# One batch of roots in place of two in the second layer normalisation of a two-block metaformer kernel

## The reference

```python
x = x + _L0_conv_ref(_ln_c(x), ...)                 # block 1, with normalisation 0 over channels
t = _to_tokens(x)
t = t + _L0_ffn_ref(_ln_t(t), ...)                  # block 2, with normalisation 1 over channels
...
def _ln_t(v, eps=1e-05):
    m = jnp.mean(v, axis=-1, keepdims=True)
    s = jnp.var(v, axis=-1, keepdims=True)
    return (v - m) / jnp.sqrt(s + eps)
# in _L0_ffn_ref: one choice of two experts per image, from the mean over the image's tokens
logits = jnp.mean(x, axis=1) @ Wr + br
routing_weights = jax.nn.softmax(logits, axis=-1)
```

## Time and profile before

| | us |
|---|---|
| median of 3 timed runs | 288.39 |
| lowest and highest | 288.17, 289.09 |
| the profiled execution, its own time | 287.14 |
| its span, first to last instruction | 285.3 |
| PE, DVE, ACT busy in the span | 269.7, 156.7, 142.0 |

### The profile page before, as it was taken

One profiled execution on the slowest core, in us unless ns is written; L12 is line 12 of the kernel. 1 busy time (PEld: TensorE's weight loads), 2 busy tenths in 40 slices (PEclk: granted clock), 3 DMA queues, 4 the chain that ended last, 5 costly groups with the idle time before them and its releaser, 6 DMA issues.

```text
span 285.3 us, 6450 instructions
## 1 busy us (share of the span) xinstructions
PE 269.7 (95%) x2474; PEld 139.5 (49%) x2474; DVE 156.7 (55%) x357; ACT 142.0 (50%) x225; POOL 33.3 (12%) x74
## 2 busy tenths in 40 slices
PE   5899999999889898999899999999999999999993
PEld 4464444346665446757355434533344444444672
DVE  3676887787753385556635148473344444444444
ACT  3642242524358665046612355265555566666672
POOL 6224546400025200000000000000000000000000
PEclk9999999999999999999999999999999999999999
DMA  7716768770000000000008980000966900800010
GB/s 189 287 48 180 217 201 227 205 267 0 0 2 1 2 1 2 2 0 2 0 20 203 209 173 1 2 0 14 191 142 142 192 0 2 177 10 2 0 39 22
DMA packets 11566, 24.09 MB, mean 84 GB/s; under 512 B 2192, under 2 KB 4400, under 8 KB 11408
## 3 DMA queue, kind: packets, MB, share of 16 engines
q1 hardware_dynamic: 9808, 19.19, 27.2%
q0 software_dynamic: 1328, 3.84, 5.4%
q10 hardware_dynamic: 400, 0.66, 0.8%
HBM read 14.73 MB, written 1.33 MB: 56 GB/s over the span
## 4 chain that ended last, share of the span: by engine, by line
PE 82%; DVE 9%; ACT 3%; issue 3%; DMA 2%; DVEq 1%; ACTq 0%; POOLq 0%
PE PS L803 21%; PE PS L780 21%; PE PS L735 6%; PE PS L610 6%; PE PS L506 4%; PE PS L562 3%; PE PS L540 3%; PE PS L708 2%; PE PS L690 2%; PE PS L627 2%; PE PS L599 2%; PE PS L575 2%; DMA X<-x_in 2%; PE PS L634 2%; PE PS L749 2%
## 5 line engine op out<-in xcount | busy, mean ns | idle before, releaser
L780 PE MATMUL PS<-N,late 64*64 64x512 f32 (+1 forms) x640 | 70.8, 550 | 0.0
L942 ACT ACTIVATE amp<-PS,late 128x1024 f32<-128x1024 f32 (+1 forms) x40 | 39.0, 1025 | 32.2 <-PE PS L780 32.2
L942 ACT ACTIVATE h<-PS,late 128x1024 f32<-128x1024 f32 (+1 forms) x40 | 39.2, 1025 | 31.8 <-PE PS L780 31.8
L780 PEld LDWEIGHTS PS<-N,late 64*64 64x64 f32 x640 | 26.1, 133 | 32.5 <-issue 31.5
L803 PE MATMUL PS<-amp,late 64*64 64x512 f32 (+1 forms) x320 | 35.3, 549 | 0.0
L803 PE MATMUL PS<-h,late 64*64 64x512 f32 (+1 forms) x320 | 35.0, 548 | 0.0
L1297 DVE SCALAR_TENSOR_TENSOR D<-PS,late,moved 128x512 f32<-128x512 f32 (+1 forms) x24 | 14.8, 657 | 28.5 <-PE PS L803 23.0
L1297 DVE SCALAR_TENSOR_TENSOR D<-PS,late,gB_odd 128x512 f32<-128x512 f32 x16 | 11.3, 747 | 28.9 <-PE PS L803 28.9
L1303 DVE TENSOR_TENSOR X<-D,X 128x512 f32<-128x512 f32 (+1 forms) x40 | 25.3, 633 | 2.1
L407 POOL DMA_DIRECT2D moved<-amp x40 | 19.7, 497 | 26.7 <-DMA moved<-amp 13.3
L844 ACT ACTIVATE Q<-PS 128x384 f32<-128x384 f32 x24 | 11.6, 488 | 21.4 <-PE PS L506 21.3
(11 more groups left out here) (151 smaller groups left out, 290.2 us busy)
## 6 DMA issues: line engine op xcount, KB each, us to landing
gB_odd<-gates_hbm SPq DMA_DIRECT2D x4, 1024.0 KB, 13.6
moved<-amp SPq DMA_DIRECT2D x40, 96.0 KB, 3.2
moved<-amp POOLq DMA_DIRECT2D x35, 96.0 KB, 2.9
moved<-gates_hbm SPq DMA_DIRECT2D x4, 512.0 KB, 7.3
moved<-gates_hbm SPq DMA_DIRECT2D x2, 1024.0 KB, 9.7
late<-late_in SPq DMA_DIRECT2D x1, 1852.0 KB, 7.5
moved<-gates_hbm SPq DMA_DIRECT2D x4, 256.0 KB, 5.4
mix<-mix_in SPq DMA_DIRECT2D x1, 897.0 KB, 9.3
```

Source lines behind the costliest of these rows:

```text
L780: mm = pe.matmul(PS[64 * r:64 * r + 64, 2 * ring(n) + half, 0:w], L("w1")[rows, u:u + 64], N[rows, a:a + w], start=True, stop=True, skip_g ...
L942: act.activation(h2[n // 2 % 2][:, 2 * (n % 2):2 * (n % 2) + 2, 0:w], pair(ring(n), w), ACT.Gelu, bias=L("b1")[:, BLOCKS * g + b:BLOCKS * ...
```

## The change

The last two batches of normalisation 1 become one, of chunks 3, 4 and 5. Its sums stand in bank 6, where those of chunks 3 and 4 stood; bank 5 no longer holds any. ACT's list takes the squares of chunks 4 and 5 ahead of their copies, and the load of the Exp table stands behind the root of the new last batch. PE's list has six unread products of 256 columns behind the sums of that batch, where there were two, three of 128 columns between the spreads of chunks 4 and 5 no longer, and three of 256 columns in place of two behind the last spread.

```diff
-BATCHES = [[[0], [1, 2], [3, 4, 5]], [[0, 1, 2], [3, 4], [5]]] + [[[0, 1, 2], [3, 4, 5]]] * 3
+BATCHES = [[[0], [1, 2], [3, 4, 5]], [[0, 1, 2], [3, 4, 5]]] + [[[0, 1, 2], [3, 4, 5]]] * 3
-SUMS_BANK = [[6, 7, 0], [7, 6, 5]]
+SUMS_BANK = [[6, 7, 0], [7, 6]]
-ROOTED = [(0, 0), (0, 1), (0, 2), (1, 0), (1, 1), (1, 2), (2, 1), (3, 0), (3, 1), (4, 0)]
+ROOTED = [(0, 0), (0, 1), (0, 2), (1, 0), (1, 1), (2, 1), (3, 0), (3, 1), (4, 0)]
...
-        root 1 1, root 1 2, warm 2, spread 1 3, spread 1 4, unread 3, spread 1 5, warm 2, route_logits, warm 2, route_loads, warm 2, route_picks, warm 4,
+        root 1 1, warm 6, spread 1 3, spread 1 4, spread 1 5, warm 3, route_logits, warm 2, route_loads, warm 2, route_picks, warm 4,
...
-                if (i, b) == (1, 2):
+                if (i, b) == (1, 1):
                     load_table(ACT.Exp)
```

More of the change, by code:

```diff
@@ L201 @@
         l1 0, l1 1, products 0 3, amplify 3, products 1 3, fc 0, fc 1, amplify 4, l1 2, l1 3, products 2 3, amplify 5, products 3 3, fc 2, fc 3, moments 1 0,
-        moments 1 1, moments 1 2, l1 4, l1 5, root 1 0, products 4 3, products 5 3, fc 4, fc 5, moments 1 3, moments 1 4, moments 1 5, root 1 1, root 1 2,
+        moments 1 1, moments 1 2, l1 4, l1 5, root 1 0, products 4 3, products 5 3, fc 4, fc 5, moments 1 3, square 1 4, square 1 5, copy 1 4, copy 1 5, root 1 1,
         router, select 0, hidden0 0, select_scaled 0, hidden0 1, hidden0 2, hidden0 3, select 1, hidden0 4, hidden0 5, select_scaled 1, hidden0 6, hidden0 7,
@@ L214 @@
         shifted 34, shifted 35, shifted 36, shifted 37, fc 2, shifted 38, shifted 39, shifted 40, l1 5, shifted 41, shifted 42, shifted 43, shifted 44,
-        shifted 45, shifted 46, shifted 47, root 1 0, fc 3, spread_l1 4, spread 1 0, spread_l1 5, spread 1 1, spread 1 2, fc 4, fc 5, center_w2, root 1 1, root 1 2,
+        shifted 45, shifted 46, shifted 47, root 1 0, fc 3, spread_l1 4, spread 1 0, spread_l1 5, spread 1 1, spread 1 2, fc 4, fc 5, center_w2, root 1 1,
         spread 1 3, spread 1 4, spread 1 5, router, down0 0 1, down0 1 1, root 2 0, spread 2 0, spread 2 1, spread 2 2, down0 2 1, down0 3 1, root 3 0, spread 3 0, spread 3 1, spread 3 2, root 2 1, conv 0, spread 2 3,
```

## The result

The changed kernel is slower. Its median is 289.59 us over twelve runs (289.01 to 290.04), against 288.42 us over twelve of the kernel before; the ratio is 1.0034, with a 95% interval of 1.0022 to 1.0046, about 0.98 us. (The two medians themselves lie 1.17 us apart; the ratio carries the interval, so I go by it.) Forecast were 288.54 us and "the same", with a range up to 289.2: the time lies outside it.

A forecast was written before the change was run, and what follows sets the result against it. PE was taken to bound most of the kernel, but DVE's chain the changed place. Spreads waiting behind unread products add 0.15 us to the 288.39 us median, giving 288.54 us; range 287.7 to 289.2, "the same" at 0.85.

The forecast's parts named there:

- the start of the sums: Sums of the one batch of chunks 3, 4 and 5 start at 71.03 us; the last sums before started at 71.75.
- the roots: In the new batch: reciprocal at 72.34 us, `rows` at 73.64; spreads could start at 73.99, 0.26 us gained at DVE's first product.
- the twelve unread records: Six unread products ahead of the spreads on PE start at 71.82 us, take 2.85 and end at 74.67.
- the wait of the spreads for them: Spreads queue behind the unread products on PE; chunk 3 is spread at 74.96 us, DVE starts at 74.99, 0.16 later than before.
- +0.15 us: Forecast cost at DVE's first product with the spread roots, carried to the end; bounds +0.07 and +0.18 us.
- the three removed DVE instructions buy nothing by themselves: At the merged batch, removing some 1.5 us of DVE busy time is worth a quarter of a microsecond at best.
- The rival by the price of the Trainium skill: Unread products ahead of the spreads, at 109 ns each, end before the roots arrive; 0.26 us gain kept, 288.1 us; chance 0.12.
- The clock as a way to slower: PE's clock falls to 1.2 GHz from its 0.57 us gap before the sums; about 3.5 us more, 291.9 us; chance 0.03.
- The rival in which the removed DVE time counts in full: Two batches of about 1.49 us become one with sums and spreads hidden: 1.5 us gained, 286.9 us; chance 0.02.
- the six records behind the last spread: Three unread products behind the last spread stream for 1.29 us, to about 76.9, just ahead of the logits at 76.99.
- the sentence behind the sum: Outside the changed place, no DMA, POOL work or SP wait changes its place; all shift with the chain.
- Another arrival of instructions: An example of effects no profile row shows, anywhere in the program, of unknown size; chance 0.09, to both sides alike.

The follow-up runs named there:

- b3: As b1, with four unread products behind the new batch's sums where the change has six: 286.45 us, ratio 0.9926.
- a3: The kernel before the change with nine unread products at its start in place of six: 287.51 us, ratio 0.9969.
- b1: The changed kernel with nine unread products at the start (as a4) and three tiny memsets more on DVE at the start: 287.37 us, ratio 0.9960.
- a4: The changed kernel with nine unread products at its start in place of six: 288.50 us, ratio 1.0000.
- b2: As a4, with one activation more on ACT at the start, so ACT's list is as long as before the change: 288.10 us, ratio 0.9989.
- c3: As a4, with two memsets more on DVE (571 instructions): one execution, 287.73 us.

## Why the prediction was wrong

**What held.** Each step at the changed place did: the start of the sums, the roots, the twelve unread records, the wait of the spreads for them, +0.15 us (measured 0.17), and also that the three removed DVE instructions buy nothing by themselves. The rival by the price of the Trainium skill ("TensorE: Matmul & The Clock Gate", section "Back-to-back issue gap"), 109 ns a product, fell: a record took 2.86 us / 12, and b3 showed what it would have been worth, 0.26 us. The prediction had also set the page's figure for a product against one record, where an f32 product here is two. The clock as a way to slower fell too: the sums behind the 0.57 us gap took 0.86 us, as in the earlier trace rows, and the trace grants the full clock from 10.47 to 286.95 us without a break. The rival in which the removed DVE time counts in full (286.9 us) fell. One term was a little off and cost nothing: the six records behind the last spread took 1.51 us, not 1.29 (by the row of four at 1.13 they come to 1.56), and the logits still start 0.14 us behind the end of `msum`, as before.

**The step that failed** is the sentence behind the sum: "No DMA, no POOL work and no SP wait changes its place; all of them shift with the chain." One kind of DMA does not shift with the chain, because it goes by the count of instructions on its engine and not by time: the loads of the instruction streams. I had counted three instructions off DVE as time (1.5 us) and not as places in its list. The last load moved from 1.4 us ahead of the last stores into them, for 0.6 to 0.8 us. With 0.17 that makes 0.8 to 1.0 us, where 0.98 was measured. "Another arrival of instructions" was named among the things unseen, with 0.09 for both sides; I could have seen that risk, though not its price, since the page lists queue 14's ten packets and a window over the last 4 us shows that one falls 1.4 us ahead of the stores.

**A smaller error** was to explain the profiled execution's 1.25 us below the median as something outside the change and leave it there. That was right, but its cause, the moment at which PE's clock rises at the start, stands in the trace. There the prediction also read the profile wrongly: the granted clock is not "full in every slice", since the trace of the kernel before has no record of it ahead of 4.61 us, and the views count time without a record as 1.00. The unread products before that moment ran at the lower pace (last section); the 1.00 for 4.20 to 5.80 us is on record from 4.61 us on. Knowing this would have changed nothing in the range: the changed kernel's median lies above all that the start explains, and above the 289.3 us of the range's own sum too.

## What to carry to other kernels

An edit that takes or adds instructions on an engine also moves that engine's later loads of instructions, here by 0.4 to 1.7 us for each instruction at the end of DVE's list; look for the load that is near something on the critical path with little to hide it, above all the last stores, and see in the trace on which side of it the load falls. If it falls on the stores, a few instructions that do nothing, placed in that engine's idle time, are worth as much as a tuned stage: here three memsets gave 0.7 us. Unread products ahead of a product that is waited for are to be costed as a row of the same form gives them, against the moment at which its operand is ready; six were 0.43 us dearer here than four.

The kernel with one batch, four unread products behind its sums, DVE's list at its old length and nine unread products at the start (b3) beats both: 286.45 us, 0.9926 of the kernel before (0.9899 to 0.9952). Most of that is not the one batch: the nine unread products alone gave 0.9969 (a3), and by the traces the one batch with four is worth 0.26 us.

## What the runs showed of the hardware

**Loads of instructions compete with stores.** They come as single packets of 8 KB (queue 14) or 16 KB (queue 8). The last ones of 8 KB took 0.31 to 0.70 us each. At the end one cost 0.6 to 0.8 us when it started 1.1 to 1.5 us behind the stores' issue; at +0.2 us it did no harm, at +0.6, where it ended just ahead of the stores' first packet, at most 0.1 us, and at +4.2 none. No run has one between +0.6 and +1.1 or between +1.5 and +4.2, and what the other loads delay in the middle of the program was not measured.

**Each engine's list moves its own load.** Queue 14 carries loads of DVE and of ACT: its last goes with DVE's number of instructions, its last but one with ACT's. Queue 8's last load comes 5.6 to 6.0 us ahead of the stores' issue in the six kernels with 2484 records on PE and 3.3 us ahead in the eight with 2474 to 2480, so it goes with PE's.

**PE's clock rises at a moment that differs from run to run.** The same records of the centring took 0.49 or 0.98 us, and the whole program 1.5 us more with the latter; with six unread products at the start both occurred for one and the same kernel. The column of the granted clock reads 1.00 in both profiles in that stretch:

```profile
5.70:8.60 2.90, 2.37 (x11) 1.26 (x11) 0.00 (x0) 0.87 (x2) 1.03 (x3) 1.00 1.12 285
```
```profile
5.70:8.60 2.90, 2.81 (x4) 1.17 (x4) 0.00 (x0) 0.87 (x2) 1.28 (x3) 1.00 1.10 291
```

The first is the kernel before, the second the changed one. The second 1.00 is no reading: the trace's first record of the granted clock begins at 4.61 us in the kernel before but only at 10.47 in the changed one, and the views count time without a record as 1.00. In every profile PE runs at half the pace until that first record and at the full pace behind it. b1, where it begins at 6.69 us, has one record of the centring on each side:

```profile
5.52 0.98 PE L507 MATMUL PS<-X,early 128*128 128x384 f32 x1
```
```profile
6.82 0.49 PE L507 MATMUL PS<-X,early 128*128 128x384 f32 x1
```

The factor is that of the clock's two levels, 1.2 and 2.4 GHz, so I take the time ahead of that record for the lower one. Such a level is on record later: in a4 (and b2) it is granted for 3.41 us from 137.5 us on (137.2 in b2), and PE gets through 20 records there, where the same stretch of b1 has 36 (a4 first, then b1). From `msum` to DVE's last instruction a4 and b2 take 206.4 us in place of 206.2; c3 takes 206.6 without such a stretch, and why stays open.

```profile
137.50:140.90 3.40, 3.40 (x20) 1.07 (x20) 3.05 (x11) 1.66 (x3) 0.00 (x0) 0.50 0.00 0
```
```profile
137.36:140.76 3.40, 3.40 (x36) 1.22 (x37) 3.05 (x11) 2.03 (x4) 0.00 (x0) 1.00 0.00 0
```

With six unread products at the start, which end by 4.2 us, the clock rose at 4.61, 4.82, 10.47, 11.80 and 11.93 us in the five profiles; with nine, which end between 4.8 and 5.5 us, between 4.04 and 7.16 in the nine. So three more unread products in the idle time before the first centring took 0.95 to 1.16 us off the medians of the two kernels; they did not make every start fast.
